# Attention's entrance in a Macaron layer: own positions for the first group and the first four chunks, another order of the chunk's steps

## The reference, cut to what matters

```
x = x + 0.5 * ffn(layernorm(x))      # gate softmax over 8 experts, top 2, + a shared expert times a sigmoid
x = x + deltanet(layernorm(x))
x = x + 0.5 * ffn(layernorm(x))      # the same weights again

def deltanet(x):                     # 16 heads of 16
    q, k, v = x@Wq, x@Wk, x@Wv       # rope on q and k
    beta = clip(sigmoid(x@Wg + bg), 0.8, 0.9995)
    pq, pk = elu(q) + 1, elu(k) + 1
    for t in tokens:                 # a scan along the sequence
        S = S*beta_t + pk_t (x) v_t;  z = z*beta_t + pk_t
        y_t = (pq_t S) / (pq_t z + eps)
    return y @ Wo + bo
```

## Time and profile before

| | us |
|---|---|
| median of 3 runs | 900.36 |
| the profiled execution, whole | 901.34 |
| its span, first to last instruction | 899.6 |
| TensorE busy | 820.8 |
| VectorE / ScalarE / GpSimd busy | 631.6 / 507.1 / 539.3 |

### The profile page before, as it was taken

The page is one execution under the profiler, slowest core; times in us unless marked ns, Lnnn a source line. Parts: engine busy times, 40 slices in busy tenths (PEclk is TensorE's granted clock), DMA queues, the critical chain, the costliest instruction groups (busy, mean ns, idle before and its releaser), DMA issues.

```text
span 899.6 us, 26468 instructions
## 1 busy us (share of the span) xinstructions
PE 820.8 (91%) x8310; PEld 752.9 (84%) x8310; DVE 631.6 (70%) x2171; ACT 507.1 (56%) x1321; POOL 539.3 (60%) x650
## 2 busy tenths in 40 slices
...
PEclk9798999999999999999999999999999999999999
...
GB/s 217 260 239 75 79 84 120 149 131 128 138 134 123 145 48 47 48 50 95 106 74 135 113 63 78 45 154 113 166 26 157 111 157 170 156 155 154 144 371 101
DMA packets 74739, 113.82 MB, mean 127 GB/s; under 512 B 9456, under 2 KB 57776, under 8 KB 73456
## 3 DMA queue, kind: packets, MB, share of 16 engines
...
...
## 4 chain that ended last, share of the span: by engine, by line
PE 30%; POOL 12%; issue 11%; ACT 5%; DVE 3%; DMA 3%; SPq 1%; DVEq 0%; another core or an unknown queue 0%; POOLq 0%; ACTq 0%
POOL expert_out L993 8%; PE PSA L1666 7%; PE PSA L1687 4%; PE PSA L1742 4%; POOL YIDX L988 3%; PE PSA L1543 3%; PE PSA L1719 2%; PE PSA L1711 2%; PE PSA L1724 2%; PE PSA L1733 2%; ACT MEM L1162 2%; PE PSA L1567 1%; PE PSA L1505 1%; ACT MEM L1175 1%; PE PSA L1674 1%
## 5 line engine op out<-in xcount | busy, mean ns | idle before, releaser
L993 POOL DMA_INDIRECT expert_out<-MEM,YIDX x142 | 148.8, 1048 | 99.8 <-ACT MEM L1135 97.1
L968 POOL DMA_INDIRECT expert_rows<-MEM,POSU x128 | 130.5, 1019 | 80.9 <-issue 33.5
L1609 PE MATMUL PSA<-EGUh,MEMR 128*128 x568 | 172.5, 345 | 6.1 <-issue 3.4
L1543 PE MATMUL PSA<-MEMR,SGUh 128*128 128x256 f32 x720 | 150.7, 294 | 1.9 <-issue 1.7
L1543 PEld LDWEIGHTS PSA<-MEMR,SGUh 128*128 128x128 f32 x720 | 117.1, 187 | 4.3 <-issue 3.9
L1609 PEld LDWEIGHTS PSA<-EGUh,MEMR 128*128 128x128 f32 x568 | 102.6, 188 | 9.9 <-issue 9.1
L1103 ACT ACTIVATE MEM<-PSA 128x256 f32<-128x256 f32 (+1 forms) x96 | 36.3, 382 | 125.9 <-PE PSA L1543 54.8
L1543 PE MATMUL PSA<-MEMR,SGUl 128*128 128x256 f32 x360 | 103.3, 287 | 0.9 <-issue 0.9
L1298 DVE TENSOR_TENSOR MEM<-PSA,MEM 128x256 f32<-128x256 f32 (+1 forms) x96 | 39.9, 418 | 75.5 <-ACT MEM L1103 43.4
L1609 PE MATMUL PSA<-EGUl,MEMR 128*128 x284 | 91.7, 323 | 0.0
L1122 ACT ACTIVATE MEM<-PSA 128x176 f32<-128x176 f32 x142 | 45.1, 318 | 73.9 <-PE PSA L1609 51.8
(11 more groups left out here) (189 smaller groups left out, 2345.4 us busy)
## 6 DMA issues: line engine op xcount, KB each, us to landing
...
```

Source lines behind the costliest of these rows:

```text
L968: pool.indirect_dma_start(out=rows_d[n.f], out_offset=bass.IndirectOffsetOnAxis(ap=POSU[:, k, i:i + 1], axis=0), in_=XN[n.xn][:, c, :], in ...
L993: pool.indirect_dma_start(out=y_d[f], out_offset=bass.IndirectOffsetOnAxis(ap=YIDX[:, j % 8:j % 8 + 1], axis=0), in_=YS[j % 3], in_offset= ...
L1543: last = mm(t[0:h, w * HALF:(w + 1) * HALF], SGU[b][:, w, k, j * P:j * P + h], XT[slot][a][:, k, hf * HALF:(hf + 1) * HALF], start=i == 0, ...
L1609: last = mm(t[:, 0:2 * HE], XGR[j % 2][a][:, k, :], EGU[b][:, bass.ds(e, 1), k, :], start=i == 0, stop=i == 3 * KD - 1)
```

## The change

Three things. First, group 0's steps (its sums, statistics, norm, transposes, `beta`, `decay`, `bias`) and chunks 0 to 3 no longer take the common offsets alone: a table `LEAD` gives them places of their own. Chunk 0 stands two positions earlier than its number says, chunks 1 and 2 about one. Second, in every chunk some offsets change, so that `state` stands directly in front of `values` and `wo` directly behind it, ahead of `back`. Third, offsets in the feed and in the second router change. SP's order does not change at all; no instruction is added or removed.

```diff
-WHEN = dict(first_sum=-9.09, ... state=0.34, ... state_sum=0.51, state_scale=1.016,
-            wo=1.937, ... xt=-4.471, ... beta=-3.09, beta_tanh=-2.69, beta_decay=-2.63, decay=-2.209, ...)
+WHEN = dict(first_sum=-9.0, ... state=0.515, ... state_sum=0.56, state_scale=1.0, wo=1.86, ... xt=-4.36, ...
+            beta=-2.487, beta_tanh=-2.3, beta_decay=-2.2, decay=-2.05, decay_read=-1.8)
-WHEN2 = dict(... xt=6.78, ... rturn=7.538, ... place=8.864, ...)
+WHEN2 = dict(... xt=6.56, ... rturn=7.37, ... place=8.62, ...)
-FEED = dict(... power=-2.485, ... xt=-2.073, ... top_tanh=-0.91, ... held=0.886, ...)
+FEED = dict(... power=-2.808, ... xt=-1.85, ... top_tanh=-1.077, ... held=1.315, ...)
+LEAD = dict(first_sum=0.91, tile_stats=0.51, stats=-2.37, power=-2.86, scale=-1.34, xt=-1.255, ...
+            bias=-0.5, chunk0=-2.0, chunk1=-0.968, chunk2=-0.976, chunk3=0.0)
...
-            put("proj", n, n, before=...)
+            chunk_at = n + LEAD.get(f"chunk{n}", 0.0)
+            put("proj", chunk_at, n, before=...)
...                                        # and so for every step of the chunk
+            lead = LEAD if g == 0 else {}
+            half, gap = (0.05, 0.1) if g == 0 else (0.25, 1.0)
+            def at(name):
+                return n + lead.get(name, 0.0)
-            put("stats", n, r, before=...)
+            put("stats", at("stats"), r, before=...)
```

More of the change, by code:

```diff
@@ L108 @@
 PLAIN_SUMS = (0, 1)
[L109 to L117, removed]
@@ L118 @@
-OWN = dict(xt_low1=0.023, xt2=-0.087, rank2=0.211, place2=0.064, place4=-0.267)
+WHEN = dict(first_sum=-9.0, scores=-0.12, mask=0.21, select=0.34, turn_copy=-0.15, back=0.88, attend=1.2, proj=-1.99, rope=-1.53, v_copy=-1.51, rope_sum=-1.02,
+            turn=-0.5, values=0.52, ocopy=0.92, wo_turn=1.48, wo_copy=1.61, state=0.515, phi_exp=-1.02, state_sum=0.56, state_scale=1.0, state_wide=1.21, wo=1.86,
+            phi=-0.8, wo_add=2.36, tile_stats=-8.46, tile_stats2=2.51, sum=-11.6, bias=-0.24, stats=-5.43, power=-4.84, scale=-4.66, xt=-4.36, xt_copy=-4.08,
+            xt_low=-3.85, beta=-2.487, beta_tanh=-2.3, beta_decay=-2.2, decay=-2.05, decay_read=-1.8)
@@ new lines @@
+WHEN2 = dict(stats=5.66, power=6.06, scale=6.34, xt=6.56, xt_copy=6.95, xt_low=6.61, gap=0.01, rout=7.09, rout_copy=7.45, rturn=7.37, top=7.88, top_tanh=8.19,
+             rank=8.63, place=8.62, scatter=9.93, every=1.08)
+FEED = dict(split=-1.732, split_every=0.287, stats=-3.076, power=-2.808, scale=-2.37, half=0.01, xt=-1.85, xt_copy=-2.09, xt_low=-2.06, gap=0.281, rout=-1.365,
+            rout_copy=-1.55, rturn=-1.3, top=-1.31, top_tanh=-1.077, rank=-0.71, place=-0.739, scatter=-0.415, every=0.2, unit=-1.254, unit_every=0.276,
+            table=3.74, ends=-4.472, slots=-1.883, blank=-1.74, fixed=3.74, held=1.315, held_every=0.187)
```

58 lines of the change are left out of this document (31 added, 27 removed).

## The result

The changed kernel takes **924.02 us** (median of 4 runs, 923.53 to 926.12), the kernel before in the same session 900.78 us (4 runs, 899.62 to 902.80): ratio **1.026**, 95% interval 1.0235 to 1.0285. It is slower by 23 us, where 2 us less were forecast.

A forecast was written before the change was run, and what follows sets the result against it. TensorE, busy 91% of the span, was taken as the bound. Terms -4.0 (feed), +6.0 (entrance), -3.4 (body), -0.5 (end of attention) sum to -1.9 us: 898.4 against 900.36, range 891.5 to 905.

The forecast's parts named there:

- The feed, -4.0: Feed before experts 0: a unit and its `down` cover the transposes' three waits for `scale`, 6.71 us in all; -4.0 us.
- later groups have DVE and ACT standing for TensorE, so it keeps: Feed, later groups: the lead of about 5 us stays, less about 1 us in group 7; value 4.0.
- The entrance, +6.0: Attention's entrance: 13.6 us idle plus 1.9 for the clock, less 6.2 idle before and 3.2 gained; taken as +6.0.
- the clock: Entrance: after the 5.8 us idle TensorE restarts at 0.50; some 3.9 us at that level cost 1.9 us.
- The body, -3.4: Body of attention: net gain of 0.6 us for each of 5.7 groups, -3.4 us; bounds -9.6 and +2.
- The term of `wo`: Body: `wo` between `values` and `back` removes two waits for `ocopy`, 0.58 and 0.85 us; -1.4 us per group of four chunks.
- `rturn`: Body: directly behind `rout`, it has to wait for ACT's copy; 0.45 us per group.
- POOL's reserve: Body: POOL has under 2 us left in 36.7 and keeps a wait of 0.81; 0.2 us taken for it.
- `beta_tanh` ... waits for `beta`, which moved behind `turn`: 0.15: Body, on ACT: `beta_tanh`, now ahead of `turn_copy` and `ocopy`, waits for `beta`; 0.15 us per group.
- `decay_read` ahead of `mask` delays DVE by 0.7 us, hidden behind `proj`: Body, on DVE: `decay_read` delays DVE by 0.7 us, hidden behind `proj`.
- The end of attention, -0.5: End of attention: idle there is chain, not order; `wo` ahead of `back` takes 0.24 and some of the last `wo`; -0.5 us.
- (a): Rival, chance 0.30: the entrance chain decides; POOL and DMA set the feed's end, so its 4.0 gain is lost; 903 us.

The follow-up runs named there:

- the block back: Changed kernel with the five numbers of beta and decay put back as before for groups 1 to 7; 1.0073 of the kernel before, body 241.55 us.
- The body's tables alone: Kernel before with only the tables of attention's body (WHEN and WHEN2) as in the change; 1.0138 of the kernel before, body 256.94 us.

## Why the prediction was wrong

**The feed, -4.0; measured +5.4 (+6.4 at the first matmul of experts 0).** The cover of the three waits was right, and three groups moved alone gain. The step that failed is "later groups have DVE and ACT standing for TensorE, so it keeps": the same number moves `xt` in all groups, and where nothing had waited, a later `xt` only brings `rout` too close behind its two copies. I priced that for group 7 alone at 1 us; TensorE's idle before the experts rose by 5.8 us (34.2 to 40.0), with `rout` +6.9 and `rturn` +2.3 against -6.1 of `xt`, and `rout(7)`, which the experts follow at a nearly fixed distance, came 6.7 us later. On the fourth and fifth chips the experts start at 137.4 to 139.0 us with the change's feed and at 135.4 to 139.4 with the others: there the whole feed order costs nothing that shows. No run moved groups 6 and 7 alone; that the loss is theirs is read from the traces.

**The entrance, +6.0; measured +8.4.** The mechanism was right almost wait for wait: before `turn(0)` 5.63 us (5.8 forecast), `turn(1)` 1.63 (1.6), `turn(2)` 2.02 (2.5), `scores(3)` 1.48 (1.7); idle time +4.0, as 13.6 - 6.2 - 3.2 said (4.2). The mis-sized term is the clock: 1.9 us taken, 4.4 us more busy time measured, since the restart lasted until about 350.5 (5.6 us at 0.50) and the gap of 2.02 us brought a second one (3.1 us at 0.50); half of the two together is 4.35. The bound of +10 named that second spell. The Trainium skill (TensorE: Matmul & The Clock Gate, section "Part 1: The HAM clock gate") has the throttled rate as the default that activity releases; by it such a gap is paid twice, and the trace agrees for two of the gaps. Behind the 1.63 us at 360.21 it does not show: from 360 to 364 the clock stays at 1.00.

```profile
360.00:364.00 4.00, 3.05 (x44) 2.46 (x44) 2.78 (x7) 3.57 (x9) 2.58 (x3) 1.00 0.29 41
```

**The body, -3.4; measured +5.5.** The term of `wo` was right in kind (-8.0 priced, about -6.4 measured), `rturn` was overpriced (+2.6 against +0.2), POOL's reserve too: with the block back the body is short again, though POOL's work is unchanged, so POOL, which carries 23% of the changed kernel's critical chain, was late and not full. What failed are the two smallest terms. "`beta_tanh` ... waits for `beta`, which moved behind `turn`: 0.15": ACT stands up to 3.0 us there (15.2 us in six groups), with the copies that `values` and `back` need behind it; putting it later alone gives 6.1 us back in the traces, 3 by the ratios. About 1.4 us of five of these waits lie behind the end that the profile gives `beta`'s last matmul, and no run shows why. And "`decay_read` ahead of `mask` delays DVE by 0.7 us, hidden behind `proj`": the 0.7 us are indeed hidden, but not the wait for the decay matmuls, which I had moved behind `scores` in the same breath; the pair alone costs 9.6 us, by a wait of `proj` that is explained and one of `ocopy` that isn't. Together 12.8, where 0.9 stood in the sum; less the 6.4 of `wo`, that is the body's loss of 5.5 within 1 us. "No wait of `back` for `ocopy`" also failed in part: 4.0 us of 12.5 stay.

**The end of attention, -0.5; measured -0.7 from `back(27)` to `back(31)`, which the body's +5.5 includes, and +3.6 behind it.** The step that failed is that nothing would move behind `back(31)`: there TensorE is idle for 2.2 us more and busy for 1.4 more, and its clock stands at 0.50 for some 8 us where it did for 3.3. What of the change does this stays open, since no experiment was made for it. The body's tables alone have it too (66.2 us and 9.5 at 0.50); on the later chips this stretch differs by 1.6 us at most (60.3 to 61.9), with or without the change.

**The rivals.** (a) had the side right, but its reason, a feed that merely doesn't gain, was not what happened, and its price, 903, was too low since it took the body's gain for safe. None of them had a body that is slower: its upper bound of +2 hung on POOL only.
